# Attention with float16 parts split once, the second batch's values made inside the loop, and the maxima moved behind the values in each step

## What is computed

```python
q = (x @ Wq).reshape(b, s, 16, 64)
k = (x @ Wk).reshape(b, s, 16, 64)
v = (x @ Wv).reshape(b, s, 16, 64)
dot = jnp.einsum('bihd,bkhd->bhik', q, k)
w = jax.nn.softmax(dot / jnp.sqrt(64.), axis=-1)
a = jnp.einsum('bhij,bjhd->bihd', w, v).reshape(b, s, 1024)
x = layernorm(x + a @ Wo + bo)
```

## Time and profile before

| | before |
|---|---|
| median of 3 runs | 928.76 us |
| the profiled execution's own time | 929.94 us |
| its span in the profile | 928.2 us |
| TensorE busy (matmuls) | 770.2 us, 83% |
| ScalarE busy | 681.2 us |
| GpSimd busy | 630.7 us |
| VectorE busy | 546.1 us |
| mean granted TensorE clock | 0.915 |

### The profile page before, as it was taken

One profiled execution on the slowest core, in us unless ns is written; L12 is line 12 of the kernel. 1 busy time (PEld: TensorE's weight loads), 2 busy tenths in 40 slices (PEclk: granted clock), 3 DMA queues, 4 the chain that ended last, 5 costly groups with the idle time before them and its releaser, 6 DMA issues. The chain is left out here.

```text
span 928.2 us, 21586 instructions
## 1 busy us (share of the span) xinstructions
PE 770.2 (83%) x9022; PEld 527.0 (57%) x9022; DVE 546.1 (59%) x881; ACT 681.2 (73%) x822; POOL 630.7 (68%) x352
## 2 busy tenths in 40 slices
PE   4788999999999999999999999999985004999500
PEld 1234666666676666666666666666664004889500
DVE  5894666766667667666666666666327601555322
ACT  3357999999999999999999999999975202444302
POOL 2406998888888888888888888889982572000174
PEclk9798999999999999999999999999995556999855
DMA  4230309113031130311303123030015011222112
GB/s 167 61 72 1 73 2 182 39 39 72 2 73 35 39 69 5 72 31 44 70 5 73 23 52 70 4 72 3 5 28 160 18 52 47 58 55 59 42 51 76
DMA packets 44287, 48.78 MB, mean 53 GB/s; under 512 B 6816, under 2 KB 28832, under 8 KB 44064
## 3 DMA queue, kind: packets, MB, share of 16 engines
q1 hardware_dynamic: 41632, 43.10, 18.9%
q0 software_dynamic: 2048, 4.23, 1.6%
q10 hardware_dynamic: 512, 0.07, 0.0%
HBM read 13.81 MB, written 8.33 MB: 24 GB/s over the span
## 5 line engine op out<-in xcount | busy, mean ns | idle before, releaser
L394 POOL TENSOR_TENSOR pl<-p,ph 128x1024 f16<-128x1024 f32 x256 | 540.9, 2133 | 114.8 <-ACT ph L325 114.4
L430 DVE TENSOR_REDUCE mx<-mps 128x1 f32<-128x1024 f32 x256 | 312.8, 1222 | 158.3 <-PE mps L195 155.9
L324 ACT ACTIVATE p<-sps,escale 128x1024 f32<-128x1024 f32 x256 | 287.1, 1122 | 38.7 <-PE sps L181 29.9
L325 ACT ACTIVATE ph<-sps,escale 128x1024 f16<-128x1024 f32 x256 | 285.6, 1116 | 0.0
L258 PE MATMUL ops<-v,ph 128*128 128x65 f16 x2048 | 214.5, 193 | 0.0
L260 PE MATMUL ops<-v,ph 128*128 128x64 f16 x2048 | 214.3, 195 | 0.0
L262 PE MATMUL ops<-v,pl 128*128 128x65 f16 x2048 | 214.0, 192 | 0.0
L258 PEld LDWEIGHTS ops<-v,ph 128*128 128x128 f16 x2048 | 190.8, 96 | 32.2 <-POOL pl L394 4.8
L260 PEld LDWEIGHTS ops<-v,ph 128*128 128x128 f16 x2048 | 190.0, 97 | 29.0
L180 PE MATMUL sps<-q_hh,k_hl 128*128 128x512 f16 x512 | 195.2, 381 | 2.9 <-ACT ph L325 2.6
L181 PE MATMUL sps<-q_lm,k_h 65*128 65x512 f16 x512 | 195.6, 382 | 0.0
(11 more groups left out here) (158 smaller groups left out, 881.0 us busy)
## 6 DMA issues: line engine op xcount, KB each, us to landing
q_hh<-hi SPq DMA_DIRECT2D x64, 128.0 KB, 2.3
q_lm<-lo SPq DMA_DIRECT2D x32, 128.0 KB, 2.4
k_hl<-hi SPq DMA_DIRECT2D x32, 128.0 KB, 2.4
k_hl<-lo SPq DMA_DIRECT2D x32, 128.0 KB, 2.4
k_h<-hi SPq DMA_DIRECT2D x32, 128.0 KB, 2.4
w<-in_w1T SPq DMA_DIRECT2D x8, 352.0 KB, 4.5
sorted<-pad SPq DMA_DIRECT2D x1, 2535.0 KB, 15.0
xb<-sorted SPq DMA_DIRECT2D x39, 65.0 KB, 2.0
```

Of the source, the lines that this page charges most:

```text
L324: nc.scalar.activation(p32[:, n % 4, :], sps[:, n % 2, :], ACT.Exp, bias=EXP_BIAS, scale=escale[:, 0:1])
L325: nc.scalar.activation(ph[:, n % 4, :], sps[:, n % 2, :], ACT.Exp, bias=EXP_BIAS, scale=escale[:, 0:1]).then_inc(s_exp, 1)
L394: nc.gpsimd.tensor_tensor(pl[:, n % 4, :], p32[:, n % 4, :], ph[:, n % 4, :], ALU.subtract).then_inc(s_subp, 1)
L430: nc.vector.tensor_reduce(mx[:, i // TB, i % TB:i % TB + 1], mps[:], AX.X, ALU.max).then_inc(s_mx, 1)
```

## The change

It has three parts.

1. **Splitting.** `x`, `Wq`, `Wk` and `Wv` are scaled and split into float16 parts once, in the prologue, before any product. Early projections and values are then three float16 products where one float32 product stood, and the projections in the loop are three float16 products where three fp32r products stood. GpSimd makes the low part of `Wv` and the low parts of the early values, for which ScalarE writes a float32 copy `v32`.
2. **Values as jobs.** The prologue makes the values of the first batch only, as 16 half tiles. The 16 half tiles of the second batch are made in the loop by a new kind of job, `values`: at step 15 of pairs 0 to 11 and at step 0 of pairs 1, 3, 5 and 7. Such a job is three matmuls, a rounding on ScalarE and a low part on VectorE.
3. **Order within a step.** TensorE does `scores(n + 3)`, `values(n)`, then `maxima(n + 14)`, then the job. VectorE's order is as before but for the new jobs.

```diff
-JOBS = {1: ("maxima", 1), 2: ("project", 0), 4: ("project", 1), 6: ("project", 2), 8: ("project", 3),
-        10: ("maxima", 0), 11: ("turn", 0), 12: ("add", 0), 13: ("turn", 1), 14: ("add", 1)}
+PRO_V = T
+
+JOBS = {0: ("values", 0), 1: ("maxima", 1), 2: ("project", 0), 4: ("project", 1), 6: ("project", 2), 8: ("project", 3),
+        10: ("maxima", 0), 11: ("turn", 0), 12: ("add", 0), 13: ("turn", 1), 14: ("add", 1), 15: ("values", 1)}
...
+        if kind == "values":
+            return pp < 12 if k else pp in (1, 3, 5, 7)
...
+            def three_products(out, a, b):
+
+                a_hi, a_lo = a
+                b_hi, b_lo = b
+                nc.tensor.matmul(out, a_hi, b_hi, start=True, stop=False)
+                nc.tensor.matmul(out, a_hi, b_lo, start=False, stop=False)
+                return nc.tensor.matmul(out, a_lo, b_hi, start=False, stop=True)
+
+            def values_of(j, out):
+
+                t, h = value_tile(j)
+                x, w = slice(t * P, (t + 1) * P), slice(h * 512, (h + 1) * 512)
+                return three_products(out, (xT_hi[:, x], xT_lo[:, x]), (w_hi[:, 2, w], w_lo[:, 2, w]))
...
-                pe.wait_ge(s_used, job)
-                nc.tensor.matmul(misc[:], wqk_hi[:, k // 2, w], xT_hi[:, x], start=True, stop=False)
-                nc.tensor.matmul(misc[:], wqk_hi[:, k // 2, w], xT_lo[:, x], start=False, stop=False)
-                nc.tensor.matmul(misc[:], wqk_lo[:, k // 2, w], xT_hi[:, x], start=False,
-                                 stop=True).then_inc(s_misc, 1)
+                return three_products(out, (w_hi[:, k // 2, w], w_lo[:, k // 2, w]), (xT_hi[:, x], xT_lo[:, x]))
...
+                if n == 0:
+                    pe.wait_ge(s_vlo, PRO_V)
...
                     n = PCH * pp + s
-                    if n + LEAD_M < PAIRS * PCH:
-                        maxima(n + LEAD_M)
                     if n + LEAD_S < PAIRS * PCH:
                         ahead, t = divmod(n + LEAD_S, PCH)
                         scores(ahead, t // CH, t % CH, n + LEAD_S)
                     values(pp, s // CH, s % CH, n)
+                    if n + LEAD_M < PAIRS * PCH:
+                        maxima(n + LEAD_M)
                     if s in jobs:
...
+                            pe.wait_ge(s_used, j)
+                            project(pp + 2, k, misc[:]).then_inc(s_misc, 1)
+                        if kind == "values":
+                            pe.wait_ge(s_used, j)
+                            values_of(value, misc[:]).then_inc(s_misc, 1)
+                            value += 1
...
+            def early_low_values(j):
+                t, h = value_tile(j)
+                rows = v[:, t, h * H // 2:(h + 1) * H // 2, :]
+                pool.wait_ge(s_v32, j + 1)
+                nc.gpsimd.tensor_tensor(rows[:, :, HD + 1:VW], v32[:, j % 4, :].rearrange("p (h c) -> p h c", c=HD),
+                                        rows[:, :, 0:HD], ALU.subtract).then_inc(s_vlo, 1)
+
+            pool.wait_ge(s_bound, 2)
+            pool.wait_ge(s_w[2], 16)
+            nc.gpsimd.tensor_scalar(w32[:], w_raw[2], scales[:, 3:4], None, ALU.mult).then_inc(s_wv32, 1)
+            pool.wait_ge(s_whi, 3)
+            pool.wait_ge(s_wv32, 1)
+            nc.gpsimd.tensor_tensor(w_lo[:, 2, :], w32[:], w_hi[:, 2, :], ALU.subtract).then_inc(s_wvlo, 1)
+            for j in range(PRO_V):
+                early_low_values(j)
...
+            def low_inputs(batch):
+                x = slice(batch * S, (batch + 1) * S)
+                dve.wait_ge(s_xhi, batch + 1)
+                nc.vector.scalar_tensor_tensor(out=xT_lo[:, x], in0=xT[:, x], scalar=scales[:, 0:1], in1=xT_hi[:, x],
+                                               op0=ALU.mult, op1=ALU.subtract).then_inc(s_xlo, 1)
...
-                    kind, k, number = jobs.get(s - 1, (None, 0, 0))
+                    kind, k, number = jobs.get(s - 1, (None, 0, 0)) if s else late
                     if kind == "maxima":
                         negate_maxima(k, job + number, 32 * pp + 16)
                     if kind == "add" and s in jobs:
                         add_output(pp - 1, k, job + number)
+                    if kind == "values" and s == 0 and s in jobs:
+                        low_values(value)
+                        value += 1
                     if n + LEAD_M < PAIRS * PCH:
                         reduce_max(n + LEAD_M)
                     if kind == "add" and s not in jobs:
                         add_output(pp - 1, k, job + number)
                     if kind == "project":
                         rest_of_piece(k, 4 * pp + 9 + k)
+                    if kind == "values" and not (s == 0 and s in jobs):
+                        low_values(value)
+                        value += 1
+                late = jobs.get(PCH - 1, (None, 0, 0))
```

More of the change, by code:

```diff
@@ L57, in first_job, with projected, value_tile @@
     return PRO_MISC + sum(len(jobs_of(i)) for i in range(pp))
+def projected(pp):
+    return first_job(pp) + 1 + max(number for kind, _, number in jobs_of(pp).values() if kind == "project")
+def value_tile(j):
+    batch, j = divmod(j, 2 * TB)
+    h, i = divmod(j, TB)
+    return batch * TB + i, h
 F_CHUNKS = [(0, 128), (128, 128), (256, 96)]
@@ L197, in maxima, with early_values, project @@
                 mm.then_inc(s_maxmm, 1)
[L199 to L211, removed]
-                                 stop=True).then_inc(s_misc, 1)
-            def project(pp, k, job):
+            def three_products(out, a, b):
[8 more added lines that the diff above has]
+                return three_products(out, (xT_hi[:, x], xT_lo[:, x]), (w_hi[:, 2, w], w_lo[:, 2, w]))
+            def early_values(j):
+                if j >= 4:
+                    pe.wait_ge(s_v32, j - 3)
+                values_of(j, sps[:, j // 2 % 2, j % 2 * 512:(j % 2 + 1) * 512]).then_inc(s_vps, 1)
+            def project(pp, k, out):
                 batch, it = divmod(pp, HALF)
@@ L347, in take_turned @@
                                      scale=vinv[:, 0:1]).then_inc(s_used, 1)
[L349 to L356, removed]
@@ new lines, in high_values, with high_weights @@
+            def high_values(j, job):
+                act.wait_ge(s_misc, job + 1)
+                nc.scalar.activation(value_rows(j), misc[:].rearrange("p (h c) -> p h c", c=HD), ACT.Copy,
+                                     scale=V_UNIT).then_inc(s_vhi, 1)
+            def high_weights(k):
+                nc.scalar.activation(w_hi[:, k, :], w_raw[k], ACT.Copy, scale=scales[:, k + 1:k + 2]).then_inc(s_whi, 1)
+            act.wait_ge(s_bound, 2)
+            nc.scalar.activation(xT_hi[:, 0:S], xT[:, 0:S], ACT.Copy, scale=scales[:, 0:1]).then_inc(s_xhi, 1)
@@ L386, in _ @@
                         take_turned(job + number)
+                    if kind == "values":
+                        high_values(value, job + number)
+                        value += 1
             act.wait_ge(s_negm, 16 * 2 * PAIRS)
@@ L430, in reduce_max, with low_values @@
                 nc.vector.tensor_reduce(mx[:, i // TB, i % TB:i % TB + 1], mps[:], AX.X, ALU.max).then_inc(s_mx, 1)
[L432 to L440, removed]
+            def low_values(j):
+                t, h = value_tile(j)
+                rows = v[:, t, h * H // 2:(h + 1) * H // 2, :]
+                dve.wait_ge(s_vhi, j + 1)
+                nc.vector.scalar_tensor_tensor(
+                    out=rows[:, :, HD + 1:VW], in0=misc[:].rearrange("p (h c) -> p h c", c=HD), scalar=V_UNIT,
+                    in1=rows[:, :, 0:HD], op0=ALU.mult, op1=ALU.subtract)\
+                    .then_inc(s_used, 1)
             def rest_of_piece(k, pieces, src=misc[:]):
@@ L473, in _, with low_weights @@
+            def low_weights(k):
+                dve.wait_ge(s_whi, k + 1)
+                nc.vector.scalar_tensor_tensor(out=w_lo[:, k, :], in0=w_raw[k], scalar=scales[:, k + 1:k + 2],
+                                               in1=w_hi[:, k, :], op0=ALU.mult, op1=ALU.subtract).then_inc(s_wlo, 1)
             nc.vector.memset(v[:, :, :, HD:HD + 1].rearrange("p t h o -> p (t h) o"), 1.0).then_inc(s_ones, 1)
-            for k, (loaded, part) in enumerate(((s_wq, wqk[:, 0, :]), (s_xT, xT[:]), (s_wk, wqk[:, 1, :]), (s_wv, wv))):
+            for column, loaded, part in ((1, s_w[0], w_raw[0]), (0, s_xT, xT), (2, s_w[1], w_raw[1]), (3, s_w[2], w_raw[2])):
@@ L482, in _ @@
             dve.wait_ge(s_bound, 1)
-            nc.vector.tensor_tensor(bound[:], bound[:], shares[:], ALU.mult).then_inc(s_bound, 1)
+            nc.vector.reciprocal(scales[:], bound[:]).then_inc(s_bound, 1)
             dve.wait_ge(s_bound, 2)
-            nc.vector.tensor_scalar(bound[:], bound[:], 1e-30, None, ALU.max).then_inc(s_bound, 1)
-            dve.wait_ge(s_bound, 3)
-            nc.vector.reciprocal(scales[:], bound[:]).then_inc(s_bound, 1)
-            dve.wait_ge(s_bound, 4)
+            low_inputs(0)
@@ L489, in _ @@
+            low_weights(0)
+            low_weights(1)
```

(11 more changed lines are left out.)

143 lines of the change are left out of this document (76 added, 67 removed).

## The result

The changed kernel takes 1036.12 us (median of 4 runs, 1031.48 to 1038.43) beside 928.32 us for the kernel before: a ratio of 1.1137, 95% interval 1.1096 to 1.1178. It is 11% slower; 1024 us was forecast, in a range of 1003 to 1047. The profiled execution took 1033.83 us, with a span of 1032.1 us, 103.9 more than before.

What follows compares the result with a forecast made beforehand. TensorE, never idle in the loop, was taken as the bound, so every wait is paid in full. Loop +105.2 and prologue -10 on the profiled 929.9 gave 1025.1; forecast 1024 us, range for 8 in 10 1003 to 1047.

Steps and rivals of the forecast that it cites:

- The mechanism: Loop: maxima behind values make the next unit's values wait for reduction, then normalisation, on VectorE; all waits together 102.4 us.
- A boundary's chain: Unit boundary: 3.85 us from maxima to next values, TensorE there after 2.05; wait 1.80, 28 times at steps 4 and 8.
- step 12: Unit boundary without a projection's low part ahead, the turn of step 11 beside it: wait 0.67 us, 14 times.
- a new pair: Start of a pair, the values job of step 15 beside it: wait 0.49 us, 12 times, 5.9 us.
- the turn: Job of step 1, turn of the maxima, waits for the item just issued: 1.46 us, in 12 pairs 17.5.
- The work: Loop: 56 projections 0.14 us shorter each, 7.6 less; 16 values jobs of 0.65 us each, 10.4 more.
- The prologue: Before the loop: transfers 5 us later, last maxima start 8 to 14 us earlier; 10 us less taken.
- The contention with GpSimd: Prologue: weight splits on VectorE beside GpSimd's split of `Wv` could take some 3 us more, leaving 7 instead of 10.
- a rival of 12%: Clock falls in the loop at half of the 28 long waits: 14 x 2 = 28 us more, 1052 us; chance 12%.
- 105.2: Whole loop: waits 102.4 plus values jobs 10.4 minus shorter projections 7.6, so +105.2 us.
- part of the chain overlaps: Boundaries cost 1.14 us instead of 1.80, the turn 1.0 instead of 1.46: 26 less, 998 us; chance 14%.
- no long wait appears: Normalisation free to run before maxima are reduced: loop changes by +2.8, 921.5 us at the median; chance 5%.

Runs made afterwards that it cites:

- the order undone: Changed kernel with TensorE's step put back to maxima, scores, values; splits, float16 parts and values jobs stay: 924.9 us, ratio 0.9949.
- the order alone: Kernel before with only TensorE's order changed to scores, values, maxima in each step: 1069.35 us, ratio 1.1491.

## Why the prediction was right, and where it was off

**The mechanism** was right: the order put the reduction of a unit's last step behind its values, the normalisation behind that reduction in VectorE's list, and the next unit's values behind both. Moving the normalisation ahead took 71 us away without touching TensorE's list.

**The sizes of the waits.** A boundary's chain measured 3.88 us (321.44 to 325.32) for 3.85, and TensorE would have come at 2.04, so the wait is 1.84 for 1.80. Two of its terms were off and nearly cancelled: the low part took 0.59 until the next instruction where 0.66 was taken, and from the product's end (325.17) to the next values 0.15 passed, where the handover was put at 0.05. At step 12 the wait was 0.82 for 0.67, at a new pair 0.60 for 0.49, at the turn 1.48 for 1.46, with a values job ahead of it 2.17 for 2.13. Pair 4, which has no fall, grew by 6.45 us (45.50 for 39.05), just what the terms give for it. That is in part luck: its waits are some 0.3 us longer than taken, and its other steps as much shorter. The range speaks of 64 boundaries and turns; by the prediction's own list there are 60 and 16.

**The work** came out nearly as said: with the order undone a values job adds 0.65 us to its step, and a step with a projection takes 2.69 us for 2.84, so 0.15 less where 0.14 was taken.

**The prologue** gave 11.6 us where 10 was taken, inside its bounds of 8 to 14. The first subtraction of GpSimd came at 65.37 where about 67 was said. The contention with GpSimd that was weighed there had no chance to come: VectorE's three splits took 1.2 to 1.3 us each and ended at about 21.3 us, before GpSimd began its own at 22.68. The last stretch of the prologue again ran at half clock, and this time it reached 3.6 us into the loop. What follows the loop took 1.5 us more, which the sum had at nothing; by chance it nearly cancels the 1.6 that the prologue gave beyond the 10.

**The step that was off** is the one that took the clock to stay at 1.00 in the loop. That it falls was made a rival of 12%, priced at 14 falls of 2 us, behind half of the 28 long waits at steps 4 and 8. What happened lies between: 4 falls in the profiled execution, none of them directly behind one of those 28 waits, at 1.6 us each, some 6.5 us. The term "105.2" for the loop measured 114.0. These falls are 6.5 of the 8.8 between them, and the half clock of the prologue, which reached into the loop, is up to 1.8 more. The profiled execution lies 8.7 us above the 1025.1 of the sum. The median of the runs lies 12 us above the forecast, since it is 2.3 above that execution where 1.2 below was taken. Slower runs had a lower mean clock (0.913 at 1038.4 us, 0.922 at 1031.48), which fits more falls in them, but only one execution has a trace.

**The rivals.** That part of the chain overlaps did not happen: the boundary's chain is unbroken, at 3.88 us. That no long wait appears would have given 922 us; the old order on TensorE gave 924.9, while another order on VectorE took away only the waits for the normalisation and gave 965.2.

**What stays open**: why a wait brings a fall in some pairs and not in others, which no run was made to tell. The changed kernel has 60 waits for the normalisation and 16 of the turn, and 4 falls. The kernel with the order alone has 15. That is some 16 of the 28 us between the order's cost there (139) and in the changed kernel (111); the rest is waits at the start of a pair, which a values job beside them shortens.

## What to carry to other kernels

When an instruction is moved within one engine's list, look for who follows it in the lists of the others. A rotation of a loop body can look free on the engine that rotates, and turn work that ran ahead into work that is waited for. On a TensorE that is busy all the time a wait costs itself and, sometimes, a spell at half clock behind it; the second part is seen only in the clock of short windows. A bundle of edits needs each one measured alone: here the order's loss of 111 us hid a gain of 5.

## What the runs showed that was not expected

Waits of 1.6 to 2.0 us were enough for the clock to fall, and each fall (3.4 us long) cost 1.6 us. Filling the waits for the normalisation with products that nobody reads made the kernel 28 us faster.

The rounding on ScalarE took 597 ns for 512 columns where it had taken 691, and the low part on VectorE 682 for 743. The change there put a constant in the place of a scale read from a tile; no run makes that edit alone.

A VectorE instruction on two columns took 1.24 us, from 26.58 to 27.82, beside a subtraction of 1024 columns on GpSimd that ended at 27.79; one on four columns with GpSimd idle took 0.17. In the kernel before, one on three columns took 1.75, until 17.11, beside a cast that ended at 17.09. In both cases the VectorE instruction ended when GpSimd's did, so it looks held up rather than slowed. The 4.21 us that the prediction reads as contention fit the same: GpSimd's sum ended at 34.15, and VectorE's subtraction 1.08 us later.
